# Two alternating PSUM banks and two fixed ones, or four shared in turn, in a fused eight-stage transformer kernel

## The reference, cut

```
layer 0  cross-attention, 16 heads of 8, key mask, 64 extra memory keys and values; output projection
layer 0  FFN 128 -> 512 -> 128 with GELU; W1 and W2 get 0.001 * outer products of 16 of the batch's own tokens
layer 1  cross-attention, q and k RMS-normed per head; output projection
layer 1  mixture of 4 experts (128 -> 512 -> 128, SiLU gate), the top 2 weighted
layer 2  cross-attention with rotary q and k; output projection
layer 2  mixture of 8 experts (352 wide), the top 2 weighted, and a shared expert (176 wide)
layer 3  cross-attention with one head of 128, no output projection
layer 3  x @ W_shared + gate-weighted x @ W_expert + bias
```

## Time and profile before

| | us |
|---|---|
| Runs of the kernel | 1090.92, 1092.05, 1089.46 |
| Median | 1090.92 |
| The profiled execution, whole | 1092.3 |
| its span in the trace | 1090.4 |
| PE busy in the span | 962.9 (88%) |
| PE weight loads | 659.4 (60%) |
| DVE busy | 572.2 (52%) |
| ACT busy | 432.6 (40%) |
| POOL busy | 270.5 (25%) |

### The profile page before, as it was taken

How to read it: one execution, slowest core, us unless ns; L and a number is a source line. 1 busy time by engine, 2 the same in 40 slices (tenths; PEclk the granted TensorE clock), 3 DMA queues, 4 the chain that set the end, 5 groups by cost and what they waited for, 6 DMA issues and landing times. The chain is left out here.

```text
span 1090.4 us, 15279 instructions
## 1 busy us (share of the span) xinstructions
PE 962.9 (88%) x5522; PEld 659.4 (60%) x5522; DVE 572.2 (52%) x1371; ACT 432.6 (40%) x777; POOL 270.5 (25%) x394
## 2 busy tenths in 40 slices
PE   2788989988689888899998889898899999999885
PEld 2544454335554443478887655444488888878783
DVE  3645555433355656455454636757453645444468
ACT  1355554442326554433333244654522423222340
POOL 7311212334425451311021023521200101010044
PEclk9989999787769999999999989989999999999997
DMA  5000000000010111000000020110000000000001
GB/s 142 4 2 13 1 15 2 13 8 10 1 63 8 33 33 32 1 22 1 1 1 1 1 73 21 39 40 15 19 1 1 1 1 1 1 1 1 1 1 39
DMA packets 27572, 18.09 MB, mean 17 GB/s; under 512 B 6221, under 2 KB 25770, under 8 KB 27370
## 3 DMA queue, kind: packets, MB, share of 16 engines
q1 hardware_dynamic: 27498, 17.12, 5.6%
HBM read 15.63 MB, written 1.05 MB: 15 GB/s over the span
## 5 line engine op out<-in xcount | busy, mean ns | idle before, releaser
L1118 DVE TENSOR_REDUCE mneg<-PS 128x2 f32<-128x308 f32 (+1 forms) x384 | 184.0, 517 | 161.6 <-PE PS L736 155.6
L1534 ACT ACTIVATE work<-PS 124x512 f32<-124x512 f32 (+1 forms) x272 | 160.4, 605 | 135.2 <-PE PS L819 134.4
L1266 DVE TENSOR_TENSOR work<-PS,work 128x512 f32<-128x512 f32 (+2 forms) x168 | 114.8, 685 | 175.5 <-PE PS L876 129.8
L1559 ACT ACTIVATE work<-PS 128x512 f32<-128x512 f32 (+2 forms) x168 | 100.1, 597 | 253.3 <-PE PS L876 240.9
L893 PEld LDWEIGHTS PS<-down_w,work 128*128 128x128 f32 (+2 forms) x1472 | 174.6, 193 | 6.2 <-DVE work L1266 1.3
L893 PE MATMUL PS<-down_w,work 128*128 128x128 f32 (+2 forms) x1472 | 174.8, 276 | 1.0 <-DVE work L1266 1.0
L874 PE MATMUL PS<-xh_sb,arena 128*128 128x512 f32 (+2 forms) x352 | 148.7, 422 | 10.4 <-DVE work L1266 9.6
L1629 POOL TENSOR_SCALAR rstd<-bn_mv 128x4 f32<-128x4 f32 x32 | 8.7, 271 | 537.7 <-DVE bn_mv L1038 537.6
L876 PE MATMUL PS<-xh_sb,arena 128*128 128x512 f32 (+2 forms) x352 | 141.7, 403 | 0.0
L875 PE MATMUL PS<-xl_sb,arena 128*128 128x512 f32 (+2 forms) x352 | 141.0, 400 | 0.0
L736 PE MATMUL PS<-kb_sb,qxt_sb 97*128 97x308 f32 x256 | 88.6, 394 | 19.6 <-DVE mneg L1118 14.9
(11 more groups left out here) (169 smaller groups left out, 1209.7 us busy)
## 6 DMA issues: line engine op xcount, KB each, us to landing
ctx_rep<-in_ctxT SPq DMA_DIRECT2D x12, 308.0 KB, 3.2
stage<-in_w SPq DMA_DIRECT2D x8, 256.0 KB, 3.6
stage<-in_wg SPq DMA_DIRECT2D x8, 176.0 KB, 2.4
stage<-in_wu SPq DMA_DIRECT2D x8, 176.0 KB, 2.9
x_res<-in_x SPq DMA_DIRECT2D x4, 256.0 KB, 4.0
down_w<-in_w SPq DMA_DIRECT2D x1, 1024.0 KB
down_w<-in_wd SPq DMA_DIRECT2D x8, 128.0 KB
out<-x_res SPq DMA_DIRECT2D x4, 256.0 KB, 2.3
```

The lines of the kernel that those rows point to most:

```text
L1118: dve.tensor_reduce(mneg[:, a % 2, t, h0:h0 + 2], PS[:, mx_bank(i_main, m), 0:2 * (KT0 if layer == 0 else KC)].rearrange("p (h n) -> p h n ...
L1266: dve.tensor_tensor(HH[0:rows, e % 2, j, :], PS[0:rows, 2 * (n % 2) + 1, :], SS[0:rows, n % 2, :], ALU.mult).then_inc(*sig["h"].mark((i, n)))
L1534: act.activation(P[0:rows, n % P_RING, :], PS[0:rows, n % 2, :], ACT.Exp, scale=SCALE).then_inc(*sig["p"].mark((i, n)))
L1559: act.activation(SS[0:rows, n % 2, :], PS[0:rows, bank, :], ACT.Silu).then_inc(*sig["act"].mark((i, n)))
```

## The change

Which bank a small product or a maximum goes to is no longer given by its kind. PE's program calls `take_bank` at each such piece, in the order in which it issues them, and gets the bank that was taken longest ago out of a pool: 2, 3, 4 and 5 in an A item, all eight in the prologue, 4 and 5 in every other item. `kt` takes a pair that starts at an even bank. The other engines look the bank up in `bank_of`. The scores (0, 1), the outputs (6, 7), the FFN matmuls (0 to 3) and A3's output (bank 5) keep theirs.

```diff
+        bank_of, taken_at, held = {}, {}, set()
+        def shared_banks(i_main):
+            if i_main is None:
+                return tuple(range(8))
+            return (2, 3, 4, 5) if ITEMS[i_main][0] == "A" else (4, 5)
+        def take_bank(i_main, label, pair=False):
+            pool = tuple(n for n in shared_banks(i_main) if n not in held)
+            if pair:
+                firsts = [n for n in pool if n % 2 == 0 and n + 1 in pool]
+                bank = min(firsts, key=lambda n: max(taken_at.get(n, -1), taken_at.get(n + 1, -1)))
+            else:
+                bank = min(pool, key=lambda n: taken_at.get(n, -1))
+            for n in (bank, bank + 1) if pair else (bank,):
+                taken_at[n] = len(bank_of)
+            bank_of[label] = bank
+            return bank
...
             def scores_for_max(i_main, a, m):
...
-                bank = mx_bank(i_main, m)
+                bank = take_bank(i_main, ("mx", a, m))
...
-                if bank in taken:
-                    pe.wait_ge(*taken[bank])
+                wait_for(bank)
...
-                pe.wait_ge(*taken[4])
-                pe.wait_ge(*taken[5])
+                bank = take_bank(i_main, ("kt", a), pair=True)
+                wait_for(bank)
+                wait_for(bank + 1)
...
-                taken[4] = taken[5] = sig["kb"].at((a, HL - 1))
+                taken[bank] = taken[bank + 1] = sig["kb"].at((a, HL - 1))
...
                 for n in range(2):
-                    pe.wait_ge(*taken[5])
-                    pe.matmul(PS[:, 5, :], OD[:, n, :], EBD[:, n, :], start=True, stop=True).then_inc(*sig["lora_psum"].mark((j, n)))
-                    taken[5] = sig["lora_w"].at((j, n))
+                    bank = take_bank(i_main, ("lora", j, n))
+                    wait_for(bank)
+                    pe.matmul(PS[:, bank, :], OD[:, n, :], EBD[:, n, :], start=True, stop=True).then_inc(*sig["lora_psum"].mark((j, n)))
+                    taken[bank] = sig["lora_w"].at((j, n))
```

More of the change, by code:

```diff
@@ L628, in _, with wait_for, k_proj @@
             taken = {}
-            def k_proj(a):
+            def wait_for(bank):
+                if bank in taken:
+                    pe.wait_ge(*taken[bank])
+            def k_proj(i_main, a):
                 layer, b = a // B, a % B
@@ L666, in v_blocks @@
                         pe.wait_ge(*sig["const_in"].at(0))
-                pe.wait_ge(*taken[4 + part])
+                bank = take_bank(i_main, ("v", a, part))
+                wait_for(bank)
                 for c in range(4 * part, min(4 * part + 4, chunks)):
-                    o = PS[0:rows, 4 + part, (c % 4) * D:(c % 4 + 1) * D]
+                    o = PS[0:rows, bank, (c % 4) * D:(c % 4 + 1) * D]
                     cols = slice(c * rows, (c + 1) * rows)
@@ L676, in v_blocks, with value_bias @@
                 mm.then_inc(*sig["v_psum"].mark((a, part)))
-                taken[4 + part] = sig["vb"].at((a, part))
-            def value_bias(layer):
+                taken[bank] = sig["vb"].at((a, part))
+            def value_bias(i_main, layer):
                 pe.wait_ge(*sig[f"wA_in{layer}"].at(0))
@@ L683, in value_bias, with xt @@
                     pe.wait_ge(*sig["mem_in"].at(0))
-                if 5 in taken:
-                    pe.wait_ge(*taken[5])
-                pe.matmul(PS[:, 5, 0:D], BVc[:, layer:layer + 1].to_broadcast([128, 128]), WA[:, layer % 2, 3, :],
+                bank = take_bank(i_main, ("bv", layer))
+                wait_for(bank)
+                pe.matmul(PS[:, bank, 0:D], BVc[:, layer:layer + 1].to_broadcast([128, 128]), WA[:, layer % 2, 3, :],
                           start=True, stop=True).then_inc(*sig["bv_psum"].mark(layer))
-                taken[5] = sig["bo_sum"].at(layer)
-            def xt(j):
+                taken[bank] = sig["bo_sum"].at(layer)
+            def xt(i_main, j):
                 pe.wait_ge(*sig["xn"].at(j))
@@ L740, in maxima_transposed @@
             def maxima_transposed(i_main, a, part):
-                bank, heads = mt_bank(i_main, part), mt_heads(part)
+                bank, heads = take_bank(i_main, ("mt", a, part)), mt_heads(part)
                 pe.wait_ge(*sig["mx"].at((a, N_MAX - 1 if part else N_MAX - MT_LAST - 1)))
-                pe.wait_ge(*taken[bank])
+                wait_for(bank)
                 for t in range(T):
```

125 lines of the change are left out of this document (61 added, 64 removed).

## The result

| | us | ratio to before, 95% interval |
|---|---|---|
| Before, median of 4 runs | 1090.9 | |
| Changed kernel, median of 4 runs | 1072.5 (1071.1 to 1075.6) | 0.984 (0.981 to 0.986) |
| Changed kernel, the profiled execution | 1075.6, a span of 1073.8 | |

The sign was right, the size was not.

The account below looks back on a forecast made before the run. PE, busy for 88% of the span, was taken as near its limit. Terms -24 + 17 + 10 - 7 + 2 - 1.5 = -3.5 us, from 1090.9 to 1087.4 us; range 1077 to 1098.

Parts of the forecast that it names:

- The maxima: Mixed items' maxima: PE's stalls for DVE's reduction, two banks for four maxima, mostly go; -24 us, bounds -10 to -34.
- a residue for DVE: In the maxima: 6 us of stall kept, since DVE would be busy for most of two slots.
- the ends: Item ends: PE's earlier arrival is lost where ACT stands for POOL's last step on the keys; 2.6 us for two items.
- slow starts and `v`: In the maxima: gain lost where the phase starts at half clock and `v` part 0 waits for a maximum; 4 us.
- The rule of the Trainium skill that the prediction set beside it: For the maxima: using all 8 PSUM banks would leave nothing of the stall; -37 us.
- The start of the items: Nine mixed items: third `qxt` waits for the fourth copy of the keys, making line 830 1.9 us late; +17 us.
- The rival in which it is absorbed: Mixed items' starts: ACT sets the pace, so +17 becomes +5 to +8, clock as now; about 1077 us, chance .20.
- The clock: Mixed items' starts: PE stands 3.5 us in one piece, so the clock falls in all nine; +10 us (0 to +24).
- The other clock rival: Mixed items' starts: item 16's long fall (3.9 us) in most, clock term +20 and more; 1097 us, chance .22.
- `lora`: Four F0 items: the second `lora` matmul no longer waits for DVE's reading of the first; -7 us (-3.4 to -12).
- FFN items and the prologue: F items, same two banks: nothing; prologue, where the four `qxt` get banks of their own: -1.5 us (0 to -3).
- Layer 3: A3: tokens' transposes take bank 5 in two of four items and wait for DVE to read A3's output; +2 us.

Follow-up runs that it names:

- the wait alone: Kernel before, with the third and fourth query transposes of the nine mixed items also waiting for the fourth copy of the keys; 1119.4 us.

## Why the prediction missed

**The maxima: the mechanism was right, the size was not, and this is the step that failed.** It had 37 us of stall, kept 6 as a residue for DVE, 2.6 for the ends, 4 for slow starts and `v`, and came to -24. Measured are -42 in the phases and +8 in the tails, so -34.

The 37 was nearly right. In item 9, where its rows come from, eight pairs at .59 are 4.7 us, and the phase became 4.3 shorter; layer 0 gave 11.4 us where it had 9, layers 1 and 2 gave 31 where it had 28. Of these 31, 3 are not the stall: the phases of items 16 and 18 took 25.2 and 25.0 us in the kernel before, at mean granted clocks of .93 and .90, and 23.6 each in the run with two `lora` banks alone, which has the same banks in them, at 1.00. That leaves 39 for 37, by a count that hit the sum more than the pieces: the eight equal pairs left out longer stalls and the second maximum of an item, which waited for a bank too. Both stand in item 9 of the kernel before:

```profile
367.40 0.41 PE L736 MATMUL PS<-kb_sb,qxt_sb 97*128 97x308 f32 x1 [0.29 <-ACT qxt_sb L1473]
...
381.68 0.79 PE L736 MATMUL PS<-kb_sb,qxt_sb 97*128 97x308 f32 x2 [0.52 <-DVE mneg L1118]
```

What failed is the part that it took off. The rows that were to bear out the 6 us of residue, DVE busy for 24.14 of 36.27 us and idle 1.09 ahead of four maxima, spoke against it; I took the residue all the same. In the phase of the changed kernel DVE is busy for 15.41 of 20.30 us and PE for all of it; over all nine phases PE is idle for .6 us, where it was for 16.9. The 4 us for slow starts were not lost either. Against this, the ends cost 7.8 and not 2.6. Together: 2 by the count, 3 by the clock, 6 and 4 by what was taken off, less 5 at the ends, make the 10 us between -24 and -34. The rule of the Trainium skill that the prediction set beside it ("Perfetto Trace Analysis", section "Matmul Optimizations", all 8 banks) would have given -37, nearer to the truth. The traces agree with it in direction, with two, three and four banks at 236.7, 209.5 and 196.7 us of phases; but the kernel's time is the same with three and with four, and no run here gives the maxima more than four.

**The start of the items: right**, +25.6 measured against 17 + 10, and shown twice: by adding the wait (+28.7 on the kernel's time) and by taking it away (-25.9). The rival in which it is absorbed, which by its number (1077) came nearest to the result, is wrong in its reason. That ACT was busy for 6.51 of 7.00 us hid nothing, since the pace behind the pause was PE's, at half clock.

**The clock** at the starts: +10 was forecast, 8.5 is left in the changed kernel and 11 in the one with the wait alone. The falls were not all of one size (starts of 10.2 to 12.7 us), but none of the nine was spared. The size is right, one reason given for it is not: the pauses of .69 and .75 us, after which the clock was said to fall in the kernel before, stand in item 9, whose start has a granted clock of 1.00, while item 8 was at the 1.2 GHz level from its first scores on, before any pause of more than .22 us in it:

```profile
325.58 1.05 PE L720 MATMUL PS<-ident_sb,qx_sb 128*97 128x128 f32 x4
```

Four transposes in 1.05 us, where item 9 has .60 or .65, with no idle time ahead of them. The other clock rival, falls as in item 16 in all, didn't come. The rule cited with it ("TensorE: Matmul & The Clock Gate", section "A second HAM failure mode: psum-queue depth-cycling") is not borne out for the maxima: with a short pause at every second slot item 9 had a granted clock of 1.00, and without them the phase above has .97. At the starts the clock did fall with a pause, the one long one; the runs that add it and take it away show that.

**`lora`**: -7 was forecast, 2.5 and 4 were measured, neither with a precision that tells 3.4 from 5. The -7 leant on the two lists of waits (9.2 us of weight loads, 7.7 of DVE). What PE stood for it in the kernel before is 5.1 us in four pieces, .84 to 2.13, so the lower bound of four times .84 = 3.4 came close by taking the shortest for all:

```profile
PE PS L768 <- DVE qa_sb L1192: 5.1, 4, 2.1
```

**FFN items and the prologue**: forecast at nothing and -1.5. With `lora`, they are worth 14. It put them at nothing because "their waits are for readers that ended microseconds before" and the FFN items' pool has the same two banks. But short waits shrink in several places, and the clock stays up in some where it had been down (below full for 61.6 us from item 3 to 8 before, for 51.2 in the changed kernel and 41.0 where banks are shared outside attention alone); the step had no term for either. How the 14 us divide is not shown. The prologue gave nothing: 57.0 against 56.8 us.

**Layer 3**: +2 forecast, +6.6 measured. Two of the three transposes that wait were found, at 1.4 us each; the third, that of the second FFN item, takes the bank of the last A3 output and was not counted. The release of a bank is not the matmul that fills it but the reader behind it, and that stood on DVE behind twelve steps of a router (lines 1154 to 1180), 2.92 us of PE's time.

**POOL's chain at the ends**: seen, priced at 2.6 us, worth 7.8 in the tails; moving it in two items gave 5.4 of tails and 7.6 of time.

In one line: -24 for the maxima should have been -34, -8.5 outside the attention items should have been -14, and +2 should have been +6.6; +27 (25.6 measured) was right. These errors add to 10 + 1 + 5.5 - 4.6 = 12 of the 15 us by which the forecast missed; the rest is not assigned by any run. Layer 3's error ran against the others; without it the forecast would have missed by 4.6 us more.

## What to carry to other kernels

A shared pool of banks, least recently taken first, knows when a bank was taken but not how long its reader needs. Look in the order of waits for the short piece that inherits the bank of the slow one, and hold that bank out: here it turned -18 us into -44. When a stall repeats in the trace with the engine behind it idle for part of each turn, take the whole of it as gain, and then ask what the next engine at the end of the stretch waits for. A bank's release is priced by the queue its reader stands in, not by the work that filled it.

## What was not expected of the hardware

The same instructions with the same pauses ran at different clocks in two kernels. In item 3 the first scores start at 192.18 us in the kernel before and at 192.22 in the changed kernel with one `lora` bank, with pauses of .45, .49 and .60 us in the one and .45, .48 and .61 in the other; then eight matmuls of the outputs take 1.93 us in the one and 1.06 in the other. The granted clock falls at 196.3 us in the first and at 201.1 in the second:

```profile
196.63 1.93 PE L830 MATMUL PS<-work,vb_sb 125*32 125x512 f32 x8 [0.60 <-DVE work L1241]
```

```profile
196.67 1.06 PE L848 MATMUL PS<-work,vb_sb 125*32 125x512 f32 x8 [0.61 <-DVE work L1261]
```

So whether a pause of this size brings TensorE down to 1.2 GHz isn't told by the pause alone, and no run here isolates what else decides it. The earlier items differ between the two kernels, but runs of one kernel differ, too: the thirteen of the kernel before lie between 1086.3 and 1094.4 us, the shortest at a mean granted clock of .945 and the longest at .936. The stretch from item 11 to 16, in which the twelve kernels differ by little but banks, lasted from 198.8 to 207.4 us over their profiles. For a forecast of this kernel it means some us of clock in either direction for each stretch that has such pauses.
